# One-hots of four tiles by one comparison, and the maximum in five operations, in a graph kernel's messages

## The reference, cut to what matters

```python
z = jnp.concatenate([node_feats[src], node_feats[dst], edge_feats], axis=1) @ W.T + b
z = (z - mean) * rsqrt(var + BN_EPS) * gamma + beta
msg = sigmoid(z[:, :H]) * softplus(z[:, H:])
agg = zeros_like(node_feats).at[src].add(msg)
```

## Time and profile before

| | us |
|---|---|
| median of 3 runs | 3820.1 (3819.95 to 3830.05) |
| the profiled execution's own time | 3820.0 |
| its span, first to last instruction | 3818.3 |
| VectorE busy in the span | 2763.0 (72%) |
| ScalarE busy in the span | 2218.7 (58%) |
| TensorE busy in the span | 3044.3 (80%) |

### The profile page before, as it was taken

How to read it: one execution, slowest core, us unless ns; L and a number is a source line. 1 busy time by engine, 2 the same in 40 slices (tenths; PEclk the granted TensorE clock), 3 DMA queues, 4 the chain that set the end, 5 groups by cost and what they waited for, 6 DMA issues and landing times. The chain is left out here.

```text
span 3818.3 us, 83823 instructions
## 1 busy us (share of the span) xinstructions
PE 3044.3 (80%) x18854; PEld 2156.6 (56%) x18855; DVE 2763.0 (72%) x7466; ACT 2218.7 (58%) x6111; POOL 2573.1 (67%) x2634
## 2 busy tenths in 40 slices
PE   6875999999988999999999976767776577767661
PEld 2322333333336777777777765656665466666661
DVE  6567888888875555555555548999998688888787
ACT  1423999999984666666666659989996010000003
POOL 2667777777776777777777760028887677777770
PEclk8986999999999999999999997888987789888885
DMA  7433333333336888888888884557774433333321
GB/s 201 129 109 100 108 101 108 102 106 107 101 95 200 264 263 264 264 263 263 263 263 264 260 296 172 200 196 275 275 270 133 112 81 77 80 80 80 75 69 41
DMA packets 315282, 640.18 MB, mean 168 GB/s; under 512 B 54446, under 2 KB 188759, under 8 KB 306999
## 3 DMA queue, kind: packets, MB, share of 16 engines
q0 software_dynamic: 99584, 247.90, 22.8%
q1 hardware_dynamic: 173416, 267.88, 22.4%
q10 hardware_dynamic: 42192, 123.38, 8.8%
HBM read 425.59 MB, written 213.37 MB: 167 GB/s over the span
## 5 line engine op out<-in xcount | busy, mean ns | idle before, releaser
L372 POOL DMA_INDIRECT rec_d<-arena x830 | 798.9, 963 | 345.0 <-issue 335.0
L871 POOL DMA_INDIRECT arena<-b_tab,arena x880 | 832.3, 946 | 281.1 <-issue 262.3
L783 PE MATMUL psum<-arena 128*128 128x440 f16 x3360 | 720.5, 352 | 50.5 <-ACT arena L466 50.0
L892 DVE TENSOR_TENSOR arena<-psum,arena 128x512 f32<-128x512 f32 x440 | 283.5, 686 | 544.1 <-DMA arena<-b_tab,arena 303.5
L634 DVE TENSOR_SCALAR arena<-iota_t,arena 128x880 f16<-128x880 f16 x840 | 523.8, 666 | 109.6 <-PE psum L783 102.6
L982 PE MATMUL psum<-weT,arena 128*128 128x256 f32 x1760 | 545.1, 392 | 45.3 <-DVE arena L892 41.9
L466 ACT ACTIVATE arena<-arena 128x128 f16<-128x128 f16 x1680 | 561.7, 386 | 0.0
L783 PEld LDWEIGHTS psum<-arena 128*128 128x128 f16 x3360 | 288.2, 97 | 477.1 <-issue 160.6
L1596 PE MATMUL psum<-arena,x_sb 128*128 128x129 f32 x2368 | 329.4, 304 | 158.8 <-DVE x_sb L1483 105.7
L1475 DVE TENSOR_TENSOR arena<-psum,arena 128x258 f32 x880 | 374.7, 426 | 83.6 <-PE psum L1596 77.5
L985 PE MATMUL psum<-arena 128*128 x2640 | 432.5, 273 | 0.0
(11 more groups left out here) (265 smaller groups left out, 5574.7 us busy)
## 6 DMA issues: line engine op xcount, KB each, us to landing
z_d<-arena ACTq DMA_DIRECT2D x220, 512.0 KB
arena<-z_d SPq DMA_DIRECT2D x44, 2560.0 KB
arena<-rec_d SPq DMA_DIRECT2D x220, 260.0 KB
arena<-in_edge_attr SPq DMA_DIRECT2D x83, 640.0 KB, 4.8
arena<-early_d SPq DMA_DIRECT2D x36, 516.0 KB
arena<-b_tab,arena POOLq DMA_INDIRECT x880
rec_d<-arena POOLq DMA_INDIRECT x831, 2.1
early_d<-arena POOLq DMA_DIRECT2D x9, 1032.0 KB, 5.2
```

What stands on the lines that cost most here:

```text
L372: nc.gpsimd.indirect_dma_start(rec_rows, bass.IndirectOffsetOnAxis(e_idx[:, s, k:k + 1], 0), e_buf[:, s, k, :], None).then_inc(s_es[s], 16)
L783: last = nc.tensor.matmul(bank(4 + 2 * k + h)[:, 0:HALF], hot_lane[:, s, k, :], hot_tile[:, s, h * HALF:(h + 1) * HALF], start=start, stop ...
L871: nc.gpsimd.indirect_dma_start(bg[:, s, k, :], None, b_tab, bass.IndirectOffsetOnAxis(rec[:, s, k, H:H + 1].bitcast(I32), 0)).then_inc(s_b ...
```

## The change

The one-hots of a group are made by one comparison of two tensors: the row of numbers, repeated for the four tiles, and the four columns of `srcloc`, each repeated over 128 columns. The maximum is cut into five operations of 512 columns, one in each group, ahead of that group's add; the multiply comes behind the add and waits for its own piece. s_spl is raised five times a chunk, so ScalarE's wait at L1318 counts five for one: it still asks for the whole maximum of the chunk two before.

```diff
-                        wait(act, s_spl, c + (i - 1))
+                        wait(act, s_spl, CG * c + (CG * i - CG))
                         nc.scalar.activation(ex[:, i, :, :], v, ACT.Sigmoid, bias=stat[:, 5:6], scale=stat[:, 4:5]).then_inc(s_q, 1)
...
                 def hots(c, g):
                     wait(dve, s_sc, c * CG + (g - CG + 1))
-                    for k in range(YG):
-                        t = (c * CG + g) * YG + k
-                        last = nc.vector.tensor_scalar(hotf[:, g, k, :], iota1, srcloc[:, bass.ds(t, 1)], None, ALU.is_equal)
-                    last.then_inc(s_hf, 1)
+                    t = (c * CG + g) * YG
+                    nc.vector.tensor_tensor(hotf[:, g, :, :], iota1.unsqueeze(1).broadcast_to([P, YG, P]),
+                                            srcloc[:, bass.ds(t, YG)].unsqueeze(2).broadcast_to([P, YG, P]), ALU.is_equal).then_inc(s_hf, 1)
...
                     dve.wait_ge(s_lg, c + 1)
                     dve.wait_ge(s_v, c + 1)
-                    nc.vector.scalar_tensor_tensor(v, ex[:, j % 2, :, :], -1.0, v, ALU.mult, ALU.max).then_inc(s_spl, 1)
                     dve.wait_ge(s_sig, c + 1)
                     before = not (isinstance(c, int) and c == 0)
                     if before:
                         firsts = adds(c - 1)
-                    dve.wait_ge(s_spl, c + 1)
                     for g in range(CG):
-                        nc.vector.tensor_tensor(u[:, g, :], u[:, g, :], v[:, g, :], ALU.mult).then_inc(s_msgT, 1)
+                        nc.vector.scalar_tensor_tensor(v[:, g, :], ex[:, j % 2, g, :], -1.0, v[:, g, :], ALU.mult, ALU.max).then_inc(s_spl, 1)
                         if before:
                             add(c - 1, (j - 1) % CS, g, firsts[g])
+                        dve.wait_ge(s_spl, CG * c + (g + 1))
+                        nc.vector.tensor_tensor(u[:, g, :], u[:, g, :], v[:, g, :], ALU.mult).then_inc(s_msgT, 1)
                         hots(c, g)
```

## The result

The changed kernel takes **4087.8 us**, median of five runs (4084.2 to 4088.5), against 3820.1 (3818.3 to 3830.1) for the kernel before: a ratio of **1.069**, 95% interval 1.068 to 1.071. Its profiled execution took 4087.8 us, with a span of 4086.1.

The account below looks back on a forecast made before the run. VectorE and ScalarE wait for each other in a 27.32 us loop per pair; freeing ScalarE's buffers late makes it 41.1. 11 + 259 + 3 − 3 = +270 on 3820 gives 4090 us, range 4015 to 4140.

Parts of the forecast that it names:

- One-hot and pieces at 0.61: VectorE, messages: merged comparison and each piece of the maximum take 0.61 us; ends for the comparison 0.42 and 0.78.
- Even chunk: VectorE idles 3.3 us before the first add, hiding the register load; the maximum is done 13.72 us after the logarithm ends.
- Odd chunk: First add 20.2 us after t, the logarithm's end, VectorE idling 4.1; copy to add 4.08, or 2.8 with fast products.
- ScalarE's waits: ScalarE waits for the maximum twice a pair, some 5 us before the first sigmoid into ex, 9 before the second.
- Period: Message loop: maxima of even chunks stand 41.1 us apart (39.8 with fast products), against 27.4 before.
- First pair: First pair of chunks, whose even chunk has no adds: next pair at 35.8 us instead of 24.4, +11.4.
- Twenty pairs: Pairs from the third chunk to the 43rd: 20 × 41.1 = 822 us against 563 before, +259.
- Last pair: Last pair of chunks: 34.5 us before to the end of the last add; only the even chunk's step lengthens it, +3.
- The pause: The 12.5 us pause in the messages falls where VectorE waits anyway, charged at nothing; +12 if that cover were gone.
- The term that was mis-sized: Behind the messages: of GpSimd's 4.8 us wait for its own stores at most that much comes back, −3.
- TensorE that never gets quick again: Rival, chance 0.07: TensorE's slow groups of 3.2 us against VectorE's 2.42 add 4.8 us a pair, +95; 4180 us.
- The other side: Rival, chance 0.04: ScalarE's buffer waits have slack, VectorE's gain counts until ScalarE bounds, −10; 3810 us.

Follow-up runs that it names:

- kernel 4: The kernel before, no operation changed, but ScalarE's wait for the buffer of ex counts on the chunk's fifth multiply instead of its maximum; 4010.3 us.
- kernel 1: The kernel before with only the merged one-hots, the maximum still one operation at the chunk's head; 3814.9 us.
- kernel 9: The kernel before with merged one-hots, ScalarE's second scaling of v moved to VectorE, and the maximum in five pieces at the chunk's head; 3796.5 us.
- kernel 10: As kernel 9, but with the maximum in two pieces, of 1024 and 1536 columns; 3807.7 us.
- kernel 11: As kernel 9, but with the scaling on VectorE also cut into five operations of 512 columns; 3806.4 us.
- kernel 3: The changed kernel with its five pieces of the maximum all ahead of the chunk's first group; 3811.9 us.
- kernel 8: The kernel before with merged one-hots and ScalarE's second scaling of v moved to VectorE, the maximum whole at the head; 3802.8 us.

## Why the prediction was right

The time was forecast at 4090 and came to 4087.8, and the mechanism was the one that the experiments confirm: pieces that stand between the groups free ScalarE's two buffers some four groups later, and both waits bind. By its steps:

1. *One-hot and pieces at 0.61.* Measured 0.60 from start to start, each 0.68 us long (2470.60 to 2471.80 above). The ends 0.42 and 0.78 are both excluded. The estimate that the prediction made from the Trainium skill, "VectorE: DVE Perf Modes", with the formula of its section "The TRN2 errata — SBUF-src ops pay a fixed extra latency per instruction", was 0.59 for the distance; the trace agrees.
2. *Even chunk.* The idle time of about 3.3 us before the first add is there, but cut in two: 1.4 us, with the register load in them, pass between the end of the logarithm and the piece, then 2.01 before the add. The sum is 3.4, so as far as the add goes the load did hide. The list of waits puts the 10.64 to 10.70 us before the piece down to "issue", not to the logarithm as the prediction said: the load comes last, behind ScalarE's signal.
3. *Odd chunk.* First add forecast at t + 20.2 with 4.1 us of idle time; measured 4.14, after a rest of TensorE of 3.67 (forecast 3.7) from which it starts slowly. From copy to add it is 4.08 (2482.16 to 2486.24), as chosen, and not 2.8. But the ground for that choice, the length of the rest, does not decide it. After the first pair 20 rests of 3.6 to 3.7 us stand ahead of odd chunks; 16 lead to transposes of 1.08 to 1.09 us, four to 0.63 to 0.67. In kernel 4 the rests there are longer, 4.0 to 4.5 us, and 16 of 20 lead to 0.63; TensorE's timeline of kernel 4:

```profile
2466.86 0.63 PE L1524 MATMUL psum<-ident,arena 128*128 128x128 f32 x4 [4.39 <-ACT arena L1307]
```

The granted clock is 0.50, the lower level of 1.2 GHz, from 2482.88 to 2488.00 in the changed kernel, and 0.61 on the mean from 2466.86 to 2471.20 in kernel 4: there it fell later, behind the transposes, and copy to add took 3.70. So this step was right in most pairs, in part by luck; with the fast products in every pair the forecast would have been 26 us lower.
4. *ScalarE's waits* of 5 and 9 us: 5.24 and 8.90. *Period* 41.1: 2467.29 to 2508.39 is 41.10.

The sum, by VectorE's timeline of the stage's start, the pair around the pause, and the end, answering to the earlier trace rows:

```profile
2306.80 0.69 DVE L1410 SCALAR_TENSOR_TENSOR arena<-arena 128x512 f32<-128x512 f32 x1 [23.35 <-ACT arena L1327]
...
2343.87 0.69 DVE L1410 SCALAR_TENSOR_TENSOR arena<-arena 128x512 f32<-128x512 f32 x1 [10.59 <-issue]
...
2593.29 0.69 DVE L1393 TENSOR_TENSOR arena<-psum,arena 128x512 f32 x1 [1.98 <-PE psum L1537]
...
2620.97 3.18 DVE L1433 BATCH_NORM_STATS2 x_sb<-arena 128x6 f32<-128x128 f32 x16
...
2634.45 0.69 DVE L1393 TENSOR_TENSOR arena<-psum,arena 128x512 f32 x1 [0.29 <-PE psum L1537]
...
3167.36 0.69 DVE L1410 SCALAR_TENSOR_TENSOR arena<-arena 128x512 f32<-128x512 f32 x1 [10.64 <-issue]
...
3202.10 0.69 DVE L1393 TENSOR_TENSOR arena<-psum,arena 128x512 f32 x1 [0.42 <-PE psum L1537]
```

- First pair: 37.07 us, which is the forecast 35.8 and the exposed load. Twenty pairs: 823.5, forecast 822. Last pair, to the end of the add: 35.4, where 34.5 + 3 had been forecast. Together 896.0 against 621.9, +274.1; forecast +273. Here +1.3, +1.5 and −2.1 nearly cancel.
- The pause was free, as charged: the even chunks' first adds around it are 41.16 us apart, in an ordinary pair of that trace 41.07, and the wait after it shrank from 1.98 to 0.29.
- Not in the sum: the stage itself begins 2.7 us later (2306.80 against 2304.08). What delays it was not followed; in the traces of the other kernels it begins between 2301.9 and 2306.0, so it may be no more than scatter.
- **The term that was mis-sized** is the last one, −3 with at most −4.8 to be had. From the end of the last add to the first gather behind the messages there were 52.9 us (2925.99 to 2978.85); now 43.7, so −9.1. GpSimd's row, answering to the earlier trace rows, says why:

```profile
3246.53 0.97 POOL L1279 DMA_INDIRECT arena<-x_tab,arena  x1 [232.23 <-DMA x_tab<-arena]
```

The prediction read the earlier trace rows as a wait of 4.80 us of which no more could come back. But that row shows only the last wait of a queue that was late altogether: with the messages ending 277 us later the early gathers are long done (3008.9), and the gather follows the table's store. From it to the end of the span both kernels need the same (839.4 and 839.6). +274.1 + 2.7 − 9.1 is +267.7; the spans differ by 267.8. The 2.7 us that were not foreseen and the 6 us too little in the last term leave the forecast 2 us too high. That it came so near is luck in these small terms; the 20 periods, 823.5 for 822, are not.

Of the rivals, TensorE that never gets quick again would have cost 95 us more; the period at its forecast length excludes it. The other side, VectorE's gain with ScalarE as the next bound, is what kernel 1 shows: 26.81 a pair, of which −4 reaches the time; it needs the maximum's end at the head of the chunk.

## What to carry to other kernels

Before an operation is cut into pieces that are spread over a loop, look for who waits for its end: a buffer is free only at the last piece, and on an in-order queue that one wait holds up everything behind it. When two engines wait for each other, add up the loop they form link by link; busy shares fall while the time rises. And a stage that gets slower costs all of it, while one that gets faster pays only until the next queue (here GpSimd's early gathers) is late.

## What the runs showed that was not expected

**VectorE's operations on two SBUF operands hold up GpSimd's gathers.** In the kernel before, of 188 early gathers between 2545 and 2845 us 22 took over 2 us, where most take 0.94, and all 22 began while a maximum ran. GpSimd's timeline and then VectorE's, around one of them:

```profile
2602.17 1.23 POOL L1269 DMA_INDIRECT x_sb<-x_tab,l_idx  x1 [0.30 <-issue]
...
2604.28 3.26 POOL L1269 DMA_INDIRECT x_sb<-x_tab,l_idx  x1 [0.30 <-issue]
2607.84 0.94 POOL L1269 DMA_INDIRECT x_sb<-x_tab,l_idx  x1 [0.31 <-issue]
```

```profile
2601.90 0.67 DVE L1413 TENSOR_TENSOR arena<-arena 128x512 f32<-128x512 f32 x1
...
2603.88 2.81 DVE L1406 SCALAR_TENSOR_TENSOR arena<-arena 128x2560 f32<-128x2560 f32 x1
2606.72 0.69 DVE L1413 TENSOR_TENSOR arena<-arena 128x512 f32<-128x512 f32 x1
2607.33 0.68 DVE L1393 TENSOR_TENSOR arena<-psum,arena 128x512 f32 x1
```

The gather of 3.26 us began inside the maximum and ended 0.85 us after the maximum's end. The gather of 1.23 us began inside a multiply and ended 0.83 after its end; the one of 0.94 began inside an add, which reads one operand from PSUM. So it is throughout: in that stretch 61 gathers began more than 0.02 us inside a maximum (22) or a multiply (39), and all ended 0.81 to 0.87 us after that operation's end; the 53 that began inside an add took 0.94 to 0.97. What counts is where a gather begins: over the whole of the messages 18 that began up to 0.75 us before a maximum, and ran into it, took 0.94 to 1.02.

The Trainium skill, "SBUF — State Buffer", section "SBUF: two separate sides", states that an operation of VectorE with two SBUF inputs and a GpSimd operation that reads SBUF shut each other out, and that the one that starts first has the ports they share for its whole instruction. The rows agree for the gather. They don't show the other half: a maximum took 2.82 us whether a gather was running at its start or not.

This is what the theory behind kernels 9 to 11 lacked: a short operation holds a gather too, only less long. With the maximum in five at the head (kernel 3) none of 215 gathers took over 2 us, but 35 took 1.35 to 2. The merged one-hots, which read two SBUF operands like a multiply, add to these: kernels 1, 3 and 8 to 11 have 29 to 62 of them, the kernel before 7, the changed kernel, where VectorE idles more, 12. In kernels 9 and 11 VectorE has hardly any idle time left (26.14 us of work in the 26.57 of a pair of kernel 9, against 24.49 in the 27.40 of kernel 3), and 7 of some 190 gathers in each took over 2 us: these began within 0.01 us of the first of five pieces and ended only after the fifth. Others with such a start took 0.94; what decides between the two was not separated by a run.

**Prices.** The scaling with one factor and one addend per partition took 1.87 us for 2560 columns on VectorE, where 1.45 had been estimated from 6272 columns with one constant in 3.36. **The clock.** In the slower pair TensorE's mean granted clock fell from 0.87 to 0.75; after a rest of 3.67 us transposes mostly took 1.09 us instead of the 0.65 after 1.84, but not by the length of the rest alone, as kernel 4 shows above.
